# First attention of a two-layer block: the sums' PSUM bank shared from step 5 on, and batch 0's rows quantised and evicted through the window banks

## The reference, cut to what matters

```python
def _qdq(x):
    s = jnp.maximum(jnp.max(jnp.abs(x), axis=-1, keepdims=True) / 127.0, 1e-08)
    return jnp.clip(jnp.round(x / s), -127.0, 127.0) * s
...
attn = jax.nn.softmax(jnp.einsum('bnhd,bmhd->bhnm', q, k) * scale, axis=-1)
o = jnp.einsum('bhnm,bmhd->bnhd', attn, v).reshape(B, N, C)
out = _qdq(o) @ _qdq(wp).T + bp
...
x = x + _L0_xattn_ref(_layernorm(x, axis=-1), ctx_2048, ...)
x = x + _L0_ffn_ref(_layernorm(x, axis=-1), L0_ffn_W1, L0_ffn_W2)
```

## Time and profile before

| what | value |
|---|---|
| median of 3 runs | 2710.77 us |
| profiled execution, its own time | 2708.0 us |
| its span | 2706.2 us |
| busy: PE, PEld, DVE, ACT, POOL | 94%, 60%, 67%, 46%, 48% of the span |
| POOL adds of attention 0 (L1338) | 140 of 4579 ns and 16 of 4588 ns |
| exponentials of attention 0 (L1212) | 832 of 598 ns |
| window reductions (L1239) | 480 of 987 ns |

### The profile page before, as it was taken

The page is one execution under the profiler, slowest core; times in us unless marked ns, Lnnn a source line. Parts: engine busy times, 40 slices in busy tenths (PEclk is TensorE's granted clock), DMA queues, the critical chain, the costliest instruction groups (busy, mean ns, idle before and its releaser), DMA issues. The chain is left out here.

```text
span 2706.2 us, 33993 instructions
## 1 busy us (share of the span) xinstructions
PE 2535.9 (94%) x13257; PEld 1635.0 (60%) x13272; DVE 1819.8 (67%) x2486; ACT 1241.7 (46%) x1869; POOL 1293.3 (48%) x337
## 2 busy tenths in 40 slices
PE   8999999998999999999977999999799999997998
PEld 7888888885444444454434777787433333334776
DVE  5564544466667666676775666654699999997764
ACT  3222222213556656556643222222588888883211
POOL 0000000003999999999970000000499999995310
PEclk9999999999999999999999999999899999998999
DMA  8777666565453543534304644444997777774200
GB/s 294 234 240 253 248 243 245 190 197 130 88 106 64 108 86 72 118 69 91 101 1 167 229 149 167 140 144 114 206 191 166 164 170 163 162 206 129 79 32 32
DMA packets 218433, 405.11 MB, mean 150 GB/s; under 512 B 18168, under 2 KB 93976, under 8 KB 218208
## 3 DMA queue, kind: packets, MB, share of 16 engines
q1 hardware_dynamic: 218272, 402.93, 53.9%
HBM read 260.63 MB, written 140.59 MB: 148 GB/s over the span
## 5 line engine op out<-in xcount | busy, mean ns | idle before, releaser
L1338 POOL TENSOR_TENSOR pooled<-pooled,probs 128x2048 f32<-128x2048 f32 x140 | 641.0, 4579 | 22.2 <-ACT probs L1212 2.5
L1212 ACT ACTIVATE probs<-psum 128x512 f32<-128x512 f32 (+1 forms) x832 | 459.3, 598 | 372.8 <-PE psum L1109 369.7
L1239 DVE TENSOR_REDUCE win_max<-psum 128x1 f32<-128x802 f32 x480 | 453.8, 987 | 169.4 <-PE psum L1074 169.2
L2021 DVE TENSOR_SCALAR probs<-psum,bound 128x1024 f32<-128x1024 f32 (+1 forms) x416 | 498.9, 1274 | 29.7 <-POOL pooled L2047 23.8
L1988 ACT ACTIVATE probs<-probs 128x1024 f32<-128x1024 f32 (+1 forms) x416 | 437.3, 1058 | 81.0 <-DVE probs L2021 38.9
L2047 POOL TENSOR_TENSOR pooled<-pooled,probs 128x2048 f32<-128x2048 f32 x94 | 433.2, 4609 | 13.1 <-ACT probs L1988 0.2
L1109 PE MATMUL psum<-q_st,k_st 128*128 128x512 f32 (+1 forms) x832 | 336.4, 439 | 36.2 <-ACT den_sb L1224 17.9
L253 POOL TENSOR_TENSOR r_q<-ve_q,minus_half 128x4 f32<-128x4 f32 x8 | 9.1, 1134 | 667.0 <-DVE ve_q L213 667.0
L1109 PEld LDWEIGHTS psum<-q_st,k_st 128*128 128x128 f32 (+1 forms) x832 | 149.0, 185 | 258.7 <-ACT probs L1212 177.1
L1074 PE MATMUL psum<-k_st,q_st 96*128 96x402 f32 x960 | 266.2, 358 | 6.3 <-DVE o_sb L1270 5.1
L1934 PE MATMUL psum<-q_st,k_st 128*128 128x512 f32 (+1 forms) x832 | 253.1, 430 | 17.8 <-PEq L176 8.7
(11 more groups left out here) (252 smaller groups left out, 4284.3 us busy)
## 6 DMA issues: line engine op xcount, KB each, us to landing
k_st<-k_hi SPq DMA_DIRECT2D x64, 801.0 KB, 12.1
k_st<-k_lo SPq DMA_DIRECT2D x48, 801.0 KB, 11.3
k_hi<-kt_hi SPq DMA_DIRECT2D x32, 801.0 KB, 4.3
k_lo<-kt_lo SPq DMA_DIRECT2D x32, 801.0 KB, 6.2
v_rows<-v_out SPq DMA_DIRECT2D x96, 256.0 KB
v_st<-v_rows SPq DMA_DIRECT2D x24, 768.0 KB
q_st<-q_hi SPq DMA_DIRECT2D x64, 256.0 KB, 10.9
w<-w_hi_d SPq DMA_DIRECT2D x64, 256.0 KB, 3.0
```

Of the source, the lines that this page charges most:

```text
L1212: A.activation(probs[i % NPROBS][0:rows, j, :], bank(score_banks.where["score", u, t, j])[0:rows, :], ACT.Exp, scale=1.0 / ROOT).then_inc( ...
L1239: V.tensor_reduce(win_max[:, r, j, c:c + 1], window(windows.where["max", u, i])[:, :, 0:MV], AX.XY, ALU.max).then_inc(max_done, 1)
L1338: G.tensor_tensor(pooled[u % 2][:], before[:], probs[tile(u, k) % NPROBS][:], ALU.add).then_inc(pool_added, 1)
L2021: V.tensor_scalar(probs[i % NPROBS][0:rows, half * W:half * W + W, :], window(("score", u, t, half))[0:rows], bound[0:rows, u // NG, t:t + 1],
```

## The change

1. `three_banks` holds from step 5 on, no longer from step 4.
2. `quantise_on_dve` is replaced in attention 0 by `first_maxima` (the reduction, ahead of the spread of unit 15's maxima) and `quantise` (behind it). Their intermediate results lie in the two window slots, which TensorE's program reserves with `quantising()` right behind `turn(15)`; the last pass writes the codes to `first.cols`.
3. `first_codes` moves from step 0 to step 3 of unit 15, `first_projection` and `first_rows` from step 2 to step 5, and the norm from step 4 to right behind `first_rows`.
4. `first_rows` works in the window itself, in place of the SBUF tiles `first.y`, and a window is free once the rows are done (`y_done`).
5. `root_on_pool` stands behind all adds of the unit.

```diff
-            LAST_SUM = 1
+            LAST_SUM, CODES_AT, ROWS_AT = 1, 3, 5
...
                 def three_banks(u, t):
-                    return 4 <= t < pooled_tiles(u) + LAG
+                    return 5 <= t < pooled_tiles(u) + LAG
...
+                    def quantising():
+                        for half in range(2):
+                            windows.take(("quantised", half))
+                            windows.freed_by(o_coded, 1)
...
                             M.wait_ge(*free)
-                            if half == 0:
-                                M.wait_ge(o_coded, 1)
...
-                            windows.freed_by(y_read, 2 * half + 2)
+                            windows.freed_by(y_done, 2 * half + 2)
...
-                            if now == (UNITS - 1, 0):
+                            if now == (UNITS - 2, TURN_AT):
+                                quantising()
+                            if now == (UNITS - 1, CODES_AT):
                                 first_codes()
-                            if now == (UNITS - 1, 2):
+                            if now == (UNITS - 1, ROWS_AT):
                                 first_projection()
...
+                    def first_maxima():
+                        V.wait_ge(o_landed, 16)
+                        V.wait_ge(max_done, max_window(UNITS, 0))
+                        V.tensor_reduce(quantised(0)[:, 0, 0:RT], first.cols[:], AX.X, ALU.max,
+                                        apply_absolute_value=True).then_inc(row_max, 1)
+
+                    def quantise():
+                        V.wait_ge(row_max, 1)
+                        s = own.after(V.tensor_scalar(first.step[:], quantised(0)[:, 0, 0:RT], 1.0 / 127.0, 1e-8,
+                                                      ALU.mult, ALU.max))
+                        V.wait_ge(own.sem, s)
+                        s = own.after(V.reciprocal(first.recip[:], first.step[:]))
+                        V.wait_ge(turned, 2 * UNITS)
+                        V.wait_ge(own.sem, s)
+                        for r in range(RT):
+                            s = own.after(V.tensor_scalar(quantised(r // 2)[:, r % 2, :], first.cols[:, r, :],
+                                                          first.recip[:, r:r + 1], 127.0, ALU.mult, ALU.min))
+                        for half in range(2):
+                            V.wait_ge(own.sem, s)
+                            s = own.after(V.tensor_scalar(quantised(half), quantised(half), -127.0, MAGIC,
+                                                          ALU.max, ALU.add))
+                        for half in range(2):
+                            V.wait_ge(own.sem, s)
+                            m = V.tensor_scalar(first.cols[:, 2 * half:2 * half + 2, :], quantised(half), MAGIC, None,
+                                                ALU.subtract)
+                        m.then_inc(o_coded, 1)
...
-                            y = first.y[r % 2]
-                            if r >= 2:
-                                V.wait_ge(y_done, r - 1)
-                            V.scalar_tensor_tensor(out=y[:], in0=window(windows.where["first", r // 2])[:, r % 2, :],
-                                                   scalar=first.step[:, r:r + 1], in1=first.w_row[:], op0=ALU.mult,
-                                                   op1=ALU.mult).then_inc(y_read, 1)
-                            V.wait_ge(y_read, r + 1)
-                            s = own.after(V.tensor_tensor(y[:], y[:], first.bp[:], ALU.add))
+                            y = window(windows.where["first", r // 2])[:, r % 2, :]
+                            s = own.after(V.scalar_tensor_tensor(out=y, in0=y, scalar=first.step[:, r:r + 1],
+                                                                 in1=first.w_row[:], op0=ALU.mult, op1=ALU.mult))
                             V.wait_ge(own.sem, s)
-                            V.tensor_tensor(first.rows[:, r, :], first.rows[:, r, :], y[:], ALU.add).then_inc(y_done, 1)
+                            s = own.after(V.tensor_tensor(y, y, first.bp[:], ALU.add))
+                            V.wait_ge(own.sem, s)
+                            V.tensor_tensor(first.rows[:, r, :], y, first.rows[:, r, :], ALU.add).then_inc(y_done, 1)
...
+                        if now == (UNITS - 2, TURN_AT - 1):
+                            first_maxima()
...
                         if now == (UNITS - 2, TURN_AT):
-                            V.wait_ge(o_landed, 16)
-                            for _ in quantise_on_dve(own, first.cols, first.step, first.recip, o_coded):
-                                pass
-                        if now == (UNITS - 1, 0):
+                            quantise()
+                        if now == (UNITS - 1, CODES_AT):
                             first_codes()
-                        if now == (UNITS - 1, 2):
+                        if now == (UNITS - 1, ROWS_AT):
                             first_rows()
-                        if now == (UNITS - 1, CLOSE_AT):
                             V.wait_ge(y_done, RT)
                             for _ in norm_on_dve(own, nm, first.rows, first.cols, 0, normed):
                                 pass
...
-                            if u == UNITS - 1 and k == pooled_tiles(u) - 2:
-                                root_on_pool(nm, 0)
+                    root_on_pool(nm, 0)
```

More of the change, by code:

```diff
@@ L1012, in attention_0 @@
                 nm = Norm(sbuf, sem, "first")
-                tables, o_landed, x_landed = sem("tables"), sem("o_landed"), sem("x_landed")
+                tables, o_landed, x_landed, row_max = sem("tables"), sem("o_landed"), sem("x_landed"), sem("row_max")
                 o_coded, q_ps, q_turned = sem("o_coded"), sem("q_ps"), sem("q_turned")
-                y_ps, y_read, y_done, normed = sem("y_ps"), sem("y_read"), sem("y_done"), sem("normed")
+                y_ps, y_done, normed = sem("y_ps"), sem("y_done"), sem("normed")
                 score_banks, windows = Banks((0, 1, 7)), Banks((1, 2))
@@ L1273, in closing, with quantised @@
                                         ALU.mult).then_inc(o_done, 1)
+                    def quantised(half):
+                        return window(windows.where["quantised", half])
+                    def first_maxima():
[23 more added lines that the diff above has]
+                        m.then_inc(o_coded, 1)
                     def first_codes():
```

## The result

The median of 4 runs is 2678.84 us (2676.99 to 2680.47) against 2710.89 (4 runs, 2709.06 to 2711.26): 32.05 us less, ratio 0.9884 with a 95% interval of 0.9868 to 0.9900. The forecast was 2681. The profiled execution took 2677.74, its span is 2676.0 us.

The account below looks back on a forecast made before the run. TensorE was taken to bound the kernel, through its waits in attention 0. Gains of 15.5 (regular units) and 14.5 (unit 15) take 30.0 off the profiled 2708.0: 2678.0, or 2681 as the runs' median; range 2673 to 2695.

Parts of the forecast that it names:

- Regular units: Attention 0, step 4: the score's wait for the copy of the sums goes, 1.11 us in 14 units, 15.5 us.
- the margin of 0.6 us: Step 4 on two banks: the needed exponential ends at 1343.7, ahead of the moved third score at 1344.3.
- rival A: Regular units keep their wait under another name; gain from nothing to half of 15.5, 2689 to 2696 us; chance 0.09.
- GpSimd's idle time: Regular units: 2.01 us idle before the first add shrinks to 0.9, so GpSimd still keeps up.
- Quantisation: VectorE behind the spread casts: small steps, four TENSOR_SCALARs into banks and four passes take 8.0 us, coded at 1382.
- rival B: GpSimd's adds also hold VectorE's instructions with banks; unit 15's gain shrinks to 2 us, 2693 to 2696; chance 0.07.
- Unit 15: TensorE in unit 15 loses its waits of 8.07, 1.43 and 2.96 us; gain 14.5, bounds 11.5 and 15.5.
- part 1: Sums' bank (bank 7) joins the scores from step 5 on, not step 4; 15.5 us over 14 units.
- The chain on VectorE: Unit 15's rows, statistics and norm end at 1415, ahead of the last closing at 1428.6: 13 us to spare.
- Rival C: The hold also takes rows and norm, so VectorE ends the stage: 2721 us; chance 0.04 with other slower causes.
- The sum: Regular units 15.5 plus unit 15's 14.5 give 30.0 us off the profiled 2708.0: 2678.0.

Follow-up runs that it names:

- e1: The kernel before with only the sums' bank joining from step 5 on instead of step 4: 2693.55 us, ratio 0.9942 to the kernel before.
- e2: The changed kernel with the sums' bank joining from step 4 on again, all else kept: 2695.31 us, ratio 0.9949 to the kernel before.
- e4: The changed kernel with the rows of batch 0 by way of the SBUF tiles y again: 2678.87 us, ratio 0.9885 to the kernel before.
- e3: The changed kernel with the quantisation in SBUF again, at the changed kernel's places: 2691.27 us, ratio 0.9935 to the kernel before.

## Why the prediction was right, step by step

- Regular units: forecast 15.5 us (1.11 a unit), measured 16.95 in 14. Around step 4 it is as forecast: from step 3 j2 to the closing it takes 4.53 us for 5.63, 1.10 less. The forecast left out another 0.12 a unit, between the values' products of step 12 and those of the next step 0 (3.42 us, 1309.65 to 1313.07, for 3.54 before, 1322.85 to 1326.39). It comes with the bank's line: the same stretch takes 3.41 in e1 (1306.73 to 1310.14) and 3.54 in e2 (1324.32 to 1327.86). At unit 15 the first score of step 0 now follows the last ones of step 12 at once, in one group of three, where it waited 0.45 us for an exponential before (1374.03 in the earlier trace rows):

```profile
1358.49 0.90 PE L1109 MATMUL psum<-q_st,k_st 128*65 128x512 f32 x3
```

- Two banks in step 4: no wait took the place, so the margin of 0.6 us was enough and rival A fails. GpSimd's idle time: forecast 0.9, measured 0.79.
- Quantisation: forecast 8.0 us behind the casts, measured 8.15. The form from SBUF to a bank, which no row of before had, costs 2.71 for four, forecast 2.8, and isn't held: rival B fails.
- Unit 15: forecast 14.5 to 14.7, measured 14.61. The forecast had the codes' transposes at 1388.5 without part 1. The closing in unit 14 stands 14.41 earlier (1331.94 for 1346.35), which gives 1374.1; they are at 1374.09.
- The chain on VectorE: forecast 13 us to spare; VectorE idles 13.31 ahead of the last closing (1413.57). Rival C fails, and by e4 it would fail without the banks as well. Its price also held all twelve instructions of the rows, when one of the four that read a bank ran beside an add in the kernel before (at 1407.51) and took 0.74 us, unheld.
- Behind step 6 there are 0.49 us that the sum didn't have. In step 9 of unit 15 a score waits 0.22 us for an exponential (at 1392.39), where it waited 0.71 (at 1421.89). e2 has 0.71 there too (at 1408.74) and e1 0.22, so this comes with the bank's line as well.
- The sum, 30.0 for 32.05, is thus short by what the bank's line does outside step 4. That the profiled execution came out at 2677.74 against a forecast 2678.0 is in part luck: its stage started 2.54 us late.
- What the forecast didn't ask is what each part does alone. They lean on each other by 3 us, as e1 and e2 show.

## What to carry to other kernels

If a chain of VectorE instructions runs beside a GpSimd that is nearly always busy, try it by way of PSUM where a window is free. Here each of the four products cost 0.68 us, where one in SBUF takes 0.43 unheld, and none waited. But first ask whether anyone waits for the chain: the quantisation's detour was worth 12.5 us, the same detour for the rows nothing. Test the parts of a change together as well as alone, for a part can move another engine's work to a worse place, as in e1. And look for the step in which an engine's other work is short before you add to it: the closing cost 0.8 us less a unit at step 10 than at step 4 or 7.

## What the hardware showed beyond the forecast

- A small instruction is held as well as a large one. A TENSOR_SCALAR of 4 columns, SBUF to SBUF, took 3.96 us in e3 and 1.87 in the changed kernel (L213, until GpSimd's last add ended at 1396.4), and 0.17 in e4, where no add ran. TENSOR_REDUCE and RECIPROCAL with source and output in SBUF (e3: 2.28 and 0.18 us beside adds) and the layer norm's statistics (2.47 for four in the changed kernel, beside adds) were not held in any run.
- GpSimd loses time too. In e4, where VectorE's additions have both operands in SBUF, GpSimd's five adds take 23.95 us for 23.44.
